# Final sum of the down projection: half of the token tiles added on Pool, half on VectorE

## The reference

```
def _act_fake_quant(x, clip_factor):
    scale = sigmoid(clip_factor) * max(abs(x)) / QMAX
    return clip(round(x / scale), -QMAX - 1.0, QMAX) * scale
...
    gate = einsum('bsh,ih->bsi', xq, _weight_fake_quant(w_gate))
    up   = einsum('bsh,ih->bsi', xq, _weight_fake_quant(w_up))
    h    = _act_fake_quant(silu(gate) * up, clip_down[0])
    return einsum('bsi,hi->bsh', h, _weight_fake_quant(w_down))
x = x + tanh(g_xattn[0]) * attention(layernorm(x), ctx_1024, ...)
x = x + tanh(g_ffn[0]) * ffn(layernorm(x), ...)
```

## Time and profile before

| | us |
|---|---|
| median of three runs | 619.09 (617.66 to 619.88) |
| the profiled execution | 617.96, with a span of 616.2 |
| DVE busy in the span | 532.3 (86%) |
| ACT busy in the span | 445.7 (72%) |
| POOL busy in the span | 264.1 (43%) |
| down projection, from the scale to the last transfer | about 582 to 616.2 |

### The profile page before, as it was taken

The page is one execution under the profiler, slowest core; times in us unless marked ns, Lnnn a source line. Parts: engine busy times, 40 slices in busy tenths (PEclk is TensorE's granted clock), DMA queues, the critical chain, the costliest instruction groups (busy, mean ns, idle before and its releaser), DMA issues. The chain is left out here.

```text
span 616.2 us, 18457 instructions
## 1 busy us (share of the span) xinstructions
PE 553.6 (90%) x6473; PEld 258.4 (42%) x6478; DVE 532.3 (86%) x679; ACT 445.7 (72%) x886; POOL 264.1 (43%) x372
## 2 busy tenths in 40 slices
PE   4999999799999989999999999999999973988485
PEld 2655565123434434444444444444445321333264
DVE  2799999899999879899899899899899746689888
ACT  2566777237777877797797797897897771788694
POOL 4898988700314444214214214214314210799300
PEclk9899999569999999999999999999999997899889
DMA  8659877532242234233233243253230000000035
GB/s 275 219 168 285 248 196 208 146 93 54 74 81 59 65 62 84 52 82 73 52 87 68 53 88 66 55 86 66 58 89 11 2 2 1 1 2 0 0 104 172
DMA packets 61255, 55.20 MB, mean 90 GB/s; under 512 B 11040, under 2 KB 58784, under 8 KB 61216
## 3 DMA queue, kind: packets, MB, share of 16 engines
q1 hardware_dynamic: 61216, 54.70, 34.9%
HBM read 37.62 MB, written 16.78 MB: 88 GB/s over the span
## 5 line engine op out<-in xcount | busy, mean ns | idle before, releaser
L828 ACT ACTIVATE prob<-st_ps 128x512 f32<-128x512 f32 x512 | 280.9, 596 | 70.5 <-PE st_ps L687 63.4
L887 DVE TENSOR_REDUCE negm<-mx_ps 128x2 f32<-128x1024 f32 x256 | 299.9, 1205 | 16.5 <-PE mx_ps L695 16.4
L687 PE MATMUL st_ps<-q,k 98*32 98x512 bf16 x2048 | 180.6, 382 | 4.5 <-ACT prob L828 4.1
L695 PE MATMUL mx_ps<-k,q 96*32 96x512 bf16 x2048 | 164.1, 396 | 7.1 <-DVE negm L887 3.4
L719 PE MATMUL pv_ps<-prob,v_u 128*32 128x512 f32 x1024 | 132.9, 592 | 1.4 <-ACT prob L828 1.4
L687 PEld LDWEIGHTS st_ps<-q,k 98*32 98x32 bf16 x2048 | 57.4, 95 | 95.8 <-ACT prob L828 41.9
L695 PEld LDWEIGHTS mx_ps<-k,q 96*32 96x32 bf16 x2048 | 54.3, 98 | 79.2 <-DVE negm L887 25.8
L1055 POOL TENSOR_TENSOR msplit<-negm,onesf 128x16 bf16<-128x16 f32 x32 | 7.1, 221 | 134.8 <-DVE negm L887 124.9
L1075 POOL TENSOR_TENSOR normal<-turned,recip 128x256 f32<-128x256 f32 x32 | 19.9, 620 | 80.0 <-DVE recip L901 80.0
L719 PEld LDWEIGHTS pv_ps<-prob,v_u 128*32 128x32 f32 x1024 | 31.8, 110 | 27.2 <-ACT prob L828 3.1
L298 POOL TENSOR_TENSOR parts<-work 128x512 bf16<-128x512 f32 x32 | 38.3, 1206 | 7.5 <-DVE work L286 6.0
(11 more groups left out here) (126 smaller groups left out, 712.4 us busy)
## 6 DMA issues: line engine op xcount, KB each, us to landing
qk_parts<-parts SPq DMA_DIRECT2D x96, 128.0 KB, 2.8
k<-qk_parts SPq DMA_DIRECT2D x192, 64.0 KB, 2.7
q<-qk_parts SPq DMA_DIRECT2D x192, 64.0 KB, 2.9
ctx<-in_ctxT SPq DMA_DIRECT2D x8, 512.0 KB, 4.7
X<-in_x SPq DMA_DIRECT2D x8, 512.0 KB, 8.7
out<-X SPq DMA_DIRECT2D x7, 512.0 KB, 2.9
q<-mrow SPq DMA_DIRECT2D x64, 4.0 KB, 2.5
wf<-in_w_down SPq DMA_DIRECT2D x1, 704.0 KB, 4.7
```

The lines of the kernel that those rows point to most:

```text
L687: last = nc.tensor.matmul(score_bank(i)[lo:lo + COLS, :], k6[g][:, h, kt * P + lo:kt * P + lo + COLS], q6[g][:, h, :], start=True, stop=True)
L695: last = nc.tensor.matmul(pair[lo:lo + COLS, qt % 2, :], q6[g][0:ROWS, h, qt * P + lo:qt * P + lo + COLS], k6[g][0:ROWS, h, :], start=True ...
L828: nc.scalar.activation(prob[kt % 2][:, h, :], score_bank(HPU * kt + h)[:], ACT.Exp, scale=SCALE).then_inc(exp_done, 1)
L887: nc.vector.tensor_reduce(negm[g % 2][:, lo:lo + 2], pair[:], op=ALU.max, axis=AX.X, negate=True).then_inc(mx_read, 1)
```

## The change

Of each chunk but the last, VectorE adds token tiles 0 and 1 and Pool adds tiles 2 and 3. Of the last chunk, Pool adds tiles 0 and 1 and VectorE tiles 2 and 3. Pool waits for y1_ready of the chunk and signals a new semaphore, out_half. VectorE waits for Pool's add of chunk n-2 before it evicts chunk n into the same y1 buffer. SP waits for both engines before it sends a chunk; for the last chunk it sends Pool's half when Pool is done and VectorE's when VectorE is done.

```diff
@@ scale_out (VectorE)
                     dve.wait_ge(y_ready, 2 * n + t1 // 2)
+                    if n >= 2:
+                        dve.wait_ge(out_half, n - 1)
                     nc.vector.tensor_tensor(y1[n % 2][:, t0:t1, :], y_ps[n % YR][:, t0:t1, :],
                                             dscale[:].unsqueeze(1).broadcast_to([P, t1 - t0, D]), ALU.mult).then_inc(y1_ready, 1)
@@ the order on VectorE
                     if n:
-                        residual(n - 1, 0, 4, n)
+                        residual(n - 1, 0, 2, n)
                 for i in range(2):
                     scale_out(NCH - 1, 2 * i, 2 * i + 2)
-                for i in range(2):
-                    residual(NCH - 1, 2 * i, 2 * i + 2, NCH + i)
+                residual(NCH - 1, 2, 4, NCH + 1)
@@ Pool, behind its products
+                for n in range(NCH):
+                    t = 2 if n < NCH - 1 else 0
+                    pool.wait_ge(y1_ready, n + 1)
+                    x = X[:, 4 * n + t:4 * n + t + 2, :]
+                    nc.gpsimd.tensor_tensor(x, x, y1[n % 2][:, t:t + 2, :], ALU.add).then_inc(out_half, 1)
@@ SP
-                def send(t0, t1, ready):
-                    sp.wait_ge(out_ready, ready)
+                def send(t0, t1):
                     sp.dma_start(out_v[:, t0:t1, :], X[:, t0:t1, :]).then_inc(out_done, DMA)
 
                 for n in range(NCH - 1):
-                    send(4 * n, 4 * n + 4, n + 1)
-                for i in range(2):
-                    send(4 * (NCH - 1) + 2 * i, 4 * (NCH - 1) + 2 * i + 2, NCH + i)
+                    sp.wait_ge(out_ready, n + 1)
+                    sp.wait_ge(out_half, n + 1)
+                    send(4 * n, 4 * n + 4)
+                sp.wait_ge(out_half, NCH)
+                send(4 * (NCH - 1), 4 * (NCH - 1) + 2)
+                sp.wait_ge(out_ready, NCH)
+                send(4 * (NCH - 1) + 2, 4 * NCH)
```

More of the change, by code:

```diff
@@ L1204, in build @@
         out_ready = sem("out_ready")
+        out_half = sem("out_half")
         out_done = sem("out_done")
```

## The result

The changed kernel takes 624.06 us (median of eight runs, 621.42 to 626.82) against 619.19 us: ratio 1.0077, interval 1.0057 to 1.0097. It is slower. The profiled execution took 621.84 us with a span of 620.1, against 617.96 and 616.2: +3.9 us, as forecast. The medians lie 4.9 us apart.

What follows compares the result with a forecast made beforehand. The prediction took VectorE alone to bound the down projection. Seven chunks at +0.54 us (+3.8) and +0.1 for the last chunk gave +3.9 us on 619.09, so 623.0 us, 0.63% slower, range 618.5 to 625.2.

Steps and rivals of the forecast that it cites:

- The bound: Down projection: from the first eviction VectorE alone sets the pace, 3.2 us a chunk; if relieved, until ScalarE takes over.
- The relief: VectorE's residual adds: seven shrink from four tiles to two, 7 x 0.54 = 3.8 us less, and 0.6 at the end.
- rival A: Residual after the clip: the engines do not collide, so the kernel gets faster, -3.5 us to 615.6 us; chance 0.11.
- The wait: VectorE's half residual behind the clip: it waits 1.08 us per chunk for Pool's add.
- one meeting at 98 to 102 us: Earlier stage, profile before: VectorE and Pool adds took turns, the waiting one going next; taken as model for the residual.
- its 0.14 us: Same meeting: a waiting Pool operation ends its own time less 0.14 us after VectorE's; for Pool's add, 1.13 us.
- The net of 0.54 a chunk: VectorE per chunk: saves 0.54 us of adding, waits 1.08 for Pool; seven chunks give +3.8 us.
- the end's +0.10: Last chunk: VectorE's half add waits for Pool's and ends at T + 2.58 instead of T + 2.48, +0.1 us.
- The order of the turn: After the eviction: clip, then waiting Pool add, then residual; if the residual passes first, clips wait instead, +0.55 us.
- B: Rival: Pool starts at the eviction's end, VectorE waits some 0.5 us a chunk, no change, 619.2 us; chance 0.08.
- C: Rival: dearer Pool add or late clips delay TensorE's last group, +0.93 per chunk, +6.8, 625.9 us; chance 0.05.

Runs made afterwards that it cites:

- Pool only: Kernel before, all residual adds still on VectorE, plus a Pool add of 128x512 float32 on unneeded data after every eviction: 628.22 us, ratio 1.0153.
- half only: Changed kernel with Pool's adds and the waits for out_half taken out, so half of the sum is missing: 615.12 us, ratio 0.9948.
- Pool behind the residual: Changed kernel, but Pool's add of chunks 0 to 6 waits for VectorE's half residual of the same chunk: 623.77 us, ratio 1.0086.
- Pool beside the eviction: Changed kernel, Pool's add held back until the next chunk's eviction begins (chunk 6: VectorE's residual), last chunk on VectorE alone: 618.00 us, ratio 0.9981.

## Why the prediction was right

*The bound.* VectorE sets the pace of the down projection. Shown from both sides: 1.08 us more per chunk brought 8.31 us (Pool only), and 0.54 us less brought 3.56 (half only), where ScalarE took over as the prediction said it would.

*The relief.* Forecast 7 x 0.54 us and something at the end, with what ScalarE allows between 2.8 and 4.3 us (rival A); measured 3.56 in the trace, 3.75 in the medians.

*The wait.* Forecast 1.08 us a chunk, from one meeting at 98 to 102 us; measured 1.07 to 1.11 (1.75 to 1.79, less 0.68). A Pool add that waited for a clip ends 1.12 us (594.34 to 595.46) or 1.15 us (590.50 to 591.65) after it, forecast 1.13. The prediction calls that meeting "the same pair of forms in the same order", which it is not: its waiting Pool operation was L298, which writes bfloat16 and takes 1.04 us, and it had waited for a VectorE add, not for a clip. That its 0.14 us would carry over was assumed, and it did. The net of 0.54 a chunk is 0.555, the end's +0.10 is +0.09 (2.57 us from the first half eviction to the end, against 2.48).

*The order of the turn.* The clip goes first, then Pool, then the residual, as I took it. With Pool behind the residual the price is the same, also shown (1.83 against 0.75 us for two clips). The prediction gives as the reason that whoever has waited goes next. In all eight meetings of the changed kernel Pool's add is also listed before the VectorE add that it holds up (590.38 and 590.41, 594.08 and 594.26, 615.43 and 615.98). So "the one that was issued first goes first" fits as well, and no run here separates the two.

*The rivals.* A (no collision) falls with the residuals of 1.75 to 1.79 us; its price, 615.6 us, is what the kernel takes when Pool is absent (615.12). Its mechanism, Pool beside the eviction, exists, but has to be made by a wait. B (half as long) and C (dearer, TensorE late) did not happen: each of the seven meetings with a residual costs 1.07 to 1.11 us (the eighth, at the end, 1.26 - 0.68 = 0.58, as Pool began earlier there), and TensorE's work of 5.2 us fits into 7.5.

*The size.* The trace has +3.97 us in the stage; the medians have +4.9, with 3.97 inside both intervals (+0.57% to +0.97% are 3.5 to 6.0 us). That the profiled spans differ by the forecast 3.9 to the tenth is luck: the two traces of the changed kernel agree to 0.01 us in the stage and lie 2.6 us apart where it begins, in code that the change does not touch, and two traces of the kernel before lie 1.15 us apart there. The stage is what bears the forecast out.

The other 0.9 us goes along with the granted TensorE clock of the executions. The 72 executions of the kernel before that were timed beside the variants took 2.3 us more for each 0.01 that their mean granted clock was lower. The changed kernel's sixteen had 0.954 on average, those 72 had 0.957. An estimate at equal clock, from these figures, gives about 4.2 us for the change, with an uncertainty of some 0.5. The same holds for Pool beside the eviction: 0.955 on average, and about 1.7 us faster at equal clock, where its median showed 0.9; and for Pool only: 0.951 or 0.952, 9.35 us in the medians and about 7.9 at equal clock. Why these executions were granted less clock is not shown; in the stage itself the changed kernel had 1.00 (592.80 to 600.30).

## What to carry to other kernels

Pool is no free second VectorE. Before giving it work, look up which VectorE instructions will lie beside it. Here a Pool add held up each VectorE add with two SBUF inputs and each int16 to bfloat16 clip until it was done, and it takes 1.27 us where VectorE needs 0.68 for the same elements, so the division lost. It paid only beside the VectorE evictions, which read PSUM and one SBUF operand (1.21 to 1.23 us with Pool beside them), and a semaphore put it there. Then ask what comes late instead: here a transfer at the end gave back 1.0 us of the gain, and 0.4 to 0.5 once it was split.

## What the runs showed of the hardware

- The engines did whole operations one after the other, without a sign of shared bandwidth: in the eight meetings of the changed kernel VectorE's half add ends 0.54 to 0.56 us behind Pool's add, and a full add of 1.22 us ends 1.07 to 1.09 us behind it (Pool only).
- The kind of access counts: beside a memset on Pool the add with two SBUF inputs took 0.68 us, beside an add 1.75 to 1.79. The clip lost 0.22 us to the memset's remainder.
- "Busy" includes standing still. VectorE's busy time rose by 4.0 us while its work fell by about 4.4.
